# Transposing attention probabilities in blocks of 128 flat columns, with V spread by DMA and expert chunks two slots earlier

## What is computed

```python
q, k = rms_norm(q, qn_w), rms_norm(k, kn_w)
attn = softmax(einsum('bqhd,bkhd->bhqk', q, k) / sqrt(64))      # 64 x 4 x 256 x 77
x = einsum('bhqk,bkhd->bqhd', attn, v).reshape(b, lq, 256) @ Wfc + fc_b
...
expert_out = einsum('becd,edf->becf', expert_in, We)            # 8 experts, 256 x 256 each
out = einsum('btk,btkd->btd', w, gathered)                      # w: softmax over the two best
x = x + tanh(g) * out
```

## Time and profile before

| | |
|---|---|
| median of 3 runs | 1439.17 us (1435.26 to 1442.53) |
| the profiled execution | 1435.99 us, span 1434.3 us |
| busy: PE, DVE, ACT, POOL | 98%, 77%, 65%, 53% of the span |
| granted TensorE clock, mean | 0.987 (1.00 in the steady pairs) |
| largest group | expert matmuls, 3072 of 512 columns, 788.0 us |
| probability transposes (L1276) | 512 matmuls |
| attention matmuls (`pT`, `vz`) | 768 of 256 columns |
| DMA, mean | 30 GB/s |

### The profile page before, as it was taken

The page is one execution under the profiler, slowest core; times in us unless marked ns, Lnnn a source line. Parts: engine busy times, 40 slices in busy tenths (PEclk is TensorE's granted clock), DMA queues, the critical chain, the costliest instruction groups (busy, mean ns, idle before and its releaser), DMA issues. The chain is left out here.

```text
span 1434.3 us, 27347 instructions
## 1 busy us (share of the span) xinstructions
PE 1398.4 (98%) x8448; PEld 1176.7 (82%) x8448; DVE 1110.1 (77%) x3146; ACT 931.2 (65%) x2600; POOL 765.4 (53%) x915
## 2 busy tenths in 40 slices
PE   5799999999999999999999999999999999999998
PEld 4688888888888888888888888888888888888876
DVE  6677877877878777878777878777878778878763
ACT  6666667666667666667666667666677666676652
POOL 3344565555565555565545565545565545565544
PEclk7799999999999999999999999999999999999999
DMA  4001110101110100100101100001101011101000
GB/s 150 19 2 35 35 35 9 35 27 35 35 35 8 35 28 35 35 24 20 35 27 35 35 17 26 31 32 35 35 9 35 28 35 35 35 9 35 8 23 23
DMA packets 29074, 43.65 MB, mean 30 GB/s; under 512 B 4672, under 2 KB 12288, under 8 KB 28928
## 3 DMA queue, kind: packets, MB, share of 16 engines
q1 hardware_dynamic: 28928, 41.90, 8.6%
HBM read 25.11 MB, written 16.78 MB: 29 GB/s over the span
## 5 line engine op out<-in xcount | busy, mean ns | idle before, releaser
L314 PE MATMUL bkM<-we,x2T 128*128 128x512 f32 x3072 | 788.0, 398 | 5.0 <-DVE acc_v L1020 0.6
L314 PEld LDWEIGHTS bkM<-we,x2T 128*128 128x128 f32 x3072 | 551.8, 188 | 132.7 <-ACT a_out L640 17.5
L640 ACT ACTIVATE a_out<-bkM,gate 128x256 f32<-128x256 f32 x512 | 215.5, 476 | 163.5 <-PE bkM L314 159.6
L455 POOL TENSOR_TENSOR a_sum<-a_sum,a_out 128x256 f32<-128x256 f32 x256 | 187.7, 733 | 94.5 <-ACT a_out L640 62.7
L1020 DVE SCALAR_TENSOR_TENSOR acc_v<-bkM,gate,acc_v 128x256 f32<-128x256 f32 x384 | 185.4, 483 | 56.9 <-PE bkM L314 47.8
L411 POOL TENSOR_TENSOR rstd<-ve,minus_half 128x4 f32<-128x4 f32 x64 | 64.8, 1012 | 208.0 <-DVE ve L814 208.0
L411 POOL TENSOR_TENSOR q_r<-q_ve,minus_half 128x16 f32<-128x16 f32 x32 | 93.1, 2910 | 113.0 <-DVE q_ve L899 113.0
L442 POOL TENSOR_TENSOR probs<-probs,p_inv 128x308 f32<-128x308 f32 x128 | 91.4, 715 | 82.0 <-DVE p_inv L914 82.0
L411 POOL TENSOR_TENSOR k_r<-k_ve,minus_half 77x8 f32<-77x8 f32 x32 | 52.3, 1634 | 145.8 <-DVE k_ve L863 145.8
L545 ACT ACTIVATE xn<-x_sb,shift,rstd 128x256 f32<-128x256 f32 x128 | 66.5, 590 | 76.9 <-DVE shift L823 76.9
L460 POOL TENSOR_TENSOR y<-a_sum,acc_v 128x256 f32<-128x256 f32 x128 | 94.5, 738 | 17.3 <-issue 0.4
(11 more groups left out here) (177 smaller groups left out, 2888.6 us busy)
## 6 DMA issues: line engine op xcount, KB each, us to landing
x_sb<-in_x SPq DMA_DIRECT2D x32, 512.0 KB, 3.9
out<-y SPq DMA_DIRECT2D x64, 256.0 KB, 2.0
ctx_sb<-in_ctx SPq DMA_DIRECT2D x32, 154.0 KB
stage<-in_L_ffn_We SPq DMA_DIRECT2D x2, 1024.0 KB, 6.1
stage<-in_L_xattn_Wkv SPq DMA_DIRECT2D x1, 512.0 KB, 5.4
stage<-in_L_xattn_Wq SPq DMA_DIRECT2D x1, 256.0 KB, 5.5
stage<-in_L_xattn_Wfc SPq DMA_DIRECT2D x1, 256.0 KB, 3.9
bias_bc<-in_L_xattn_fc_b SPq DMA_DIRECT2D x1, 128.0 KB, 4.9
```

Of the source, the lines that this page charges most:

```text
L314: mm = nc.tensor.matmul(out, l, r, start=(i == 0), stop=(i == len(terms) - 1))
L455: nc.gpsimd.tensor_tensor(a, o[:, 0] if i == 1 else a, o[:, i], ALU.add).then_inc(a_summed.sem, 1)
L640: ins = nc.scalar.activation(a_out[:, t % 2, (e // 4) * 2 + i], bkM[1][:, i * D:(i + 1) * D], ACT.Copy, scale=gate[:, m.parity, t, e:e + 1])
```

## The change

Four things.

1. **Transposes.** The four heads' probabilities stand side by side in `probs`, 4 x 77 = 308 flat columns. They are padded to 384 (the padding is zeroed once) and transposed as 3 blocks of 128, whatever head a column is of. Flat column 77 h + k becomes a row of block c = (77 h + k) // 128. 12 transposes per pair instead of 16, each 128 x 128. `pT` is 128 x 384 per tile instead of 77 x 512.
2. **V.** A row of a block must meet the V row of the same head and key. ACT and DVE now write V's parts plainly (`v_nat`, 77 rows), and SP moves them into `vf` by six DMAs (`put_v`): each head's 77 rows, cut where a block ends, to the partitions where the block has them, in the 64 columns of that head; the rest of `vf` is zero from the start. Half 0 needs blocks 0 and 1, half 1 blocks 1 and 2, so each output is still two products of three terms.
3. **Attention by batch.** An output bank holds one batch with both halves (before: one half with both batches). TensorE runs both halves of batch 0 in slot 14, of batch 1 in slot 15, and the projection of a batch waits for that batch alone.
4. **Chunks two slots earlier.** In slot k runs chunk k + 2 of pair m, in slots 14 and 15 chunks 0 and 1 of pair p. Chunks 0 and 1 of the first pair move into `second_round`; the last step has 14 chunks. POOL's `finish_tile` of tiles 0 and 1 moves ahead accordingly.

```diff
+V_BLOCKS = ((0, 0), (1, 0), (1, 1), (2, 1))
+def v_pieces():
+    for h in range(H):
+        row = h * LK
+        while row < (h + 1) * LK:
+            c = row // P
+            end = min((h + 1) * LK, (c + 1) * P)
+            yield V_BLOCKS.index((c, h // 2)), row - c * P, row - h * LK, end - row, h
+            row = end
+def block_rows(c):
+    return min(P, HK - c * P)
...
-        vz = sb("vz", [LK, 2, BP, KC, 2 * P], F32R)
+        v_nat = sb("v_nat", [LK, 2 * BP, D], F32R)
+        vf = sb("vf", [P, 2 * BP, len(V_BLOCKS), P], F32R)
...
+        LEAD = 2
+        def chunk_of(k, m, p):
+            c = k + LEAD
+            return (m, c) if c < SLOTS else (p, c - SLOTS)
...
+            def put_v(f):
+                sp.wait_ge(v_lo.sem, v_lo.at(f))
+                sp.sem_inc(waits_alone, 1)
+                sp.wait_ge(o_ps.sem, o_ps.before(f))
+                sp.sem_inc(waits_alone, 1)
+                for block, row, k, n, h in V_PIECES:
+                    sp.dma_start(vf[row:row + n, :, block, (h % 2) * DH:(h % 2 + 1) * DH].bitcast(F32),
+                                 v_nat[k:k + n, :, h * DH:(h + 1) * DH].bitcast(F32)).then_inc(v_put.sem, 16)
...
                 if ahead:
                     load(ahead)
+                if f:
+                    put_v(f)
                 store(m, 0)
...
             def slots(m, p, f):
                 if f:
                     ln1(f)
+                if m:
+                    finish_tile(m, 0)
                 if p:
                     ln2(p)
                 if f:
                     k_rsqrt(f)
                 if m:
-                    finish_tile(m, 0)
+                    finish_tile(m, 1)
                 if f:
                     make_xb(f, 0)
                     q_rsqrt(f)
                     make_xb(f, 1)
                     make_xb(f, 3)
-                if m:
-                    finish_tile(m, 1)
...
-                copy(pT[:, 0, t // SUB, :, t % SUB], s_bank[t][0:LK, :].rearrange("k (h q) -> k h q", h=H)
-                     ).then_inc(pT_hi.sem, 1)
+                copy(pT[:, 0, t // SUB, :, t % SUB], p_chunks(t)).then_inc(pT_hi.sem, 1)
...
-                for h in range(H):
-                    tr = pe.transpose(s_bank[t][0:LK, h * P:(h + 1) * P], probs[:, t, h * LK:(h + 1) * LK],
-                                      ident[:])
+                for c in range(PC):
+                    tr = pe.transpose(s_bank[t][:, c * P:(c + 1) * P], probs[:, t, c * P:(c + 1) * P], ident[:])
...
             def attend(f, m, b, p):
-                pe.wait_ge(v_lo.sem, v_lo.at(f))
                 if m == 0:
+                    pe.wait_ge(v_put.sem, v_put.at(f))
+                    pe.wait_ge(pT_lo.sem, pT_lo.at(f, SUB * (b + 1)))
                     if p and b == 0:
                         pe.wait_ge(x2T_lo.sem, x2T_lo.at(p))
-                    pe.wait_ge(pT_lo.sem, pT_lo.at(f, SUB * (b + 1)))
-                elif p and b == 0:
-                    pe.wait_ge(gate_chain.sem, gate_chain.at(p))
-                mm = product(o_bank[m][:, b * LQ:(b + 1) * LQ], [
-                    ([vz[:, a, b, m, j * P:(j + 1) * P] for a in range(2)],
-                     [pT[:, a, b, 2 * m + j].rearrange("k s q -> k (s q)") for a in range(2)])
-                    for j in range(2)])
+                    elif p:
+                        pe.wait_ge(gate_chain.sem, gate_chain.at(p))
+                mm = product(o_bank[b][:, m * LQ:(m + 1) * LQ], [
+                    ([vf[0:rows, a * BP + b, block] for a in range(2)],
+                     [pT[0:rows, a, b, c].rearrange("k s q -> k (s q)") for a in range(2)])
+                    for block, (c, heads) in enumerate(V_BLOCKS) if heads == m
+                    for rows in (block_rows(c),)])
...
                 if k == 14 and f:
                     attend(f, 0, 0, p)
+                    attend(f, 1, 0, p)
                 if k == 15 and f:
                     attend(f, 0, 1, p)
-                    attend(f, 1, 0, p)
                     attend(f, 1, 1, p)
```

More of the change, by code:

```diff
@@ L571, in kv @@
                                      ).then_inc(k_sq_done.sem, 1)
-                act.wait_ge(o_ps.sem, o_ps.before(f))
-                copy(vz_heads(0, b), v_heads(b)).then_inc(v_hi.sem, 1)
+                act.wait_ge(v_put.sem, v_put.before(f))
+                copy(v_nat[:, b], v_cols(b)).then_inc(v_hi.sem, 1)
             def q(f, i):
@@ L643, in experts, with chunk @@
                 ins.then_inc(a_ready.sem, 1)
+            def chunk(k, m, p):
+                pair, c = chunk_of(k, m, p)
+                if pair:
+                    experts(pair, c)
             def slot(k, m, p, f, xn_made=False):
@@ L651, in slot @@
                         ctx_hi(f)
-                    if m:
-                        experts(m, k)
+                    chunk(k, m, p)
                 if k == 3:
@@ L667, in slot @@
                         ln2(p)
-                if k == 5 and m:
-                    experts(m, k)
+                if k == 5:
+                    chunk(k, m, p)
                 if k == 6:
@@ L1420, in second_round @@
                 positions(p)
-                attend(f, 0, 0, p)
-                attend(f, 0, 1, p)
-                attend(f, 1, 0, p)
-                attend(f, 1, 1, p)
+                moe(p, 0)
+                for b in range(BP):
+                    attend(f, 0, b, p)
+                    attend(f, 1, b, p)
+                moe(p, 1)
             def fill():
```

67 lines of the change are left out of this document (40 added, 27 removed).

## The result

The changed kernel takes 1446.87 us, the median of 8 runs (1446.29 to 1451.17); the kernel before, run beside it, takes 1437.59 us (8 runs, 1435.26 to 1442.53). The ratio is 1.0072, 95% interval 1.0056 to 1.0087: slower by 0.7%, where 0.5% can be told from no change. The runs of the kernel before fall mostly into two groups, near 1436 and near 1442.4 us (in later series near 1436 and 1443), and a median depends on how many fall into each. The forecast of 1429 us has the wrong sign, and the result lies above its range. The profiled execution of the changed kernel took 1446.31 us, its span is 1444.6 us at a granted clock of 0.989.

The account below looks back on a forecast made before the run. TensorE, 98% busy, bounds the kernel, beside a DVE chain as long as its own work from slot 10 to attention. Steady pairs -9.0, shift +0.2, fill -1.3 sum to -10.1 us; 1439.17 becomes 1429 us, range 1417 to 1439.

Parts of the forecast that it names:

- The attention products: TensorE's 24 attention matmuls of 256 columns per pair: contracting 128 or 52 rows instead of 77 costed at nothing.
- rival D: Transposes: a group's cost follows the loaded columns, +0.44 us per pair, +13 us, 1452 us; chance 3%.
- Transposes, -0.45 us on TensorE: Probability transposes: 16 become 12 per pair, 4 x 0.1125 = 0.45 us off TensorE; the wider load costs nothing.
- the estimate that the prediction worked out from the Trainium skill: Transposes' weight loads: 1.0 us before, 1.3 after if loads set the pace, costing 0.3 us per pair.
- Kept 0.30 of it, DVE binds: At the first attention matmul: TensorE meets DVE's second low part, so 0.30 of 0.45 us per pair is kept, 9.0 us.
- POOL's limit: Fourth transpose group: POOL's last normalisation keeps it from starting before about 850.5, putting attention at about 852.3.
- Stall before chunk 13: Chunk 13's weights waiting for ACT's evacuation: the 0.3 us stall may go, but TensorE only arrives earlier at the same wait.
- rival A: TensorE's path alone decides: DVE's chain shrinks too, 0.45 us and the 0.3 us stall both go, 1415.6 us; chance 8%.
- The shift +0.2: Chunks two slots earlier: no work moved in steady state; drain -2.8, fill 1.4 and about 2.2, attention gain 0.6: +0.2 us.
- the fill -1.3: First two pairs: transposes cost 0.215 us each there, three groups save 0.65 us per pair, -1.3 us.
- V by DMA hidden: SP's queue: six pieces, 5 to 10 us plus issues of about 0.4 each, under 25.5 us of cover; costed at nothing.
- the dear end: V's DMA at the upper packet price of 68 ns: 1,232 packets take 5.3 us on sixteen engines, 84 on one.

Follow-up runs that it names:

- the kernel with 128 rows: The changed kernel with its last block of 52 rows contracted over all 128 rows (zero padding): 1420.96 us against 1437.16, ratio 0.9878.
- the split kernel: The changed kernel with all blocks at 128 rows, and DVE's two low parts moved ahead of the last three gate instructions: 1412.08 us, ratio 0.9813.

## Why the prediction was wrong

The step that failed is in "The attention products": "I cost that at nothing: the columns are the same, and none of the rows above goes by the contracted rows". Its cost is 0.71 us per pair by the starts in the timeline and 0.78 us by the kernel with 128 rows, some 23 us in all by the spans and 26 by the medians; the prediction's sum held it at nothing. The reasoning had a gap that can be named. All rows quoted for it contracted 77 or 128 rows; for 52 I had no row near, and took the column count for the whole price instead of bounding it. The kernel before did have a nearer row, the logits' transposes of 16 rows at 0.34 us for four, which costs more than its columns explain.

The sentence behind it failed too: "boundaries with expert chunks are as many as before". I counted boundaries between tiles and not between kinds of product, and those went from none in the attention to four per pair. None of the rivals held such a mechanism: D priced the loaded columns of the transposes, and the only slower cases had 8% between them.

The Trainium skill has a page that speaks to it, and I had not drawn on it: "TensorEngine Tiling (Array Packing)", Key Properties, says that changing the tiling mode drains TensorE, and under Performance Considerations it puts contraction sizes of 64 or less under row tiling. The step between 64 and 77 rows and the 0.195 to 0.21 us per switch would fit that; that a product of 52 rows changes the mode in this kernel is argued, and no run here shows it. The Trainium skill ("TensorE: Matmul & The Clock Gate", LDWEIGHTS) also says that a weight load's time goes by columns and not by rows. The trace agrees for the load by itself, 0.18 us with 52 rows and 0.19 with 128; at the edges of the short block the load is not hidden all the same.

The other steps, in order. One more row is needed for them, the start of DVE's chain behind chunk 10 in the changed kernel:

```profile
809.60 0.48 DVE L1068 SCALAR_TENSOR_TENSOR acc_v<-bkM,gate,x 128x256 f32<-128x256 f32 x1 [1.00 <-PE bkM L339]
```

- **Transposes, -0.45 us on TensorE: right.** The first two groups of three start 0.36 us apart, 0.12 each. The wider load costs nothing; rival D falls. So does the estimate that the prediction worked out from the Trainium skill ("TensorE: Matmul & The Clock Gate", LDWEIGHTS).
- **Kept 0.30 of it, DVE binds: right in mechanism.** Low parts of 384 columns take 0.55 us, as forecast, and the attention starts 0.10 us behind the second. Moving DVE's gates gave 0.33 us per pair, which shows that DVE held it. With 128 rows the period is 42.82, 0.42 below before: the term was 0.12 us per pair too small. POOL's limit was nearer than I made it: it costs 0.34 us ahead of the fourth group.
- **Stall before chunk 13: "may well go", it went.** 0.36 us per pair, and as I had said TensorE waits elsewhere instead: for POOL ahead of the fourth group, and longer for DVE at the attention. From the start of DVE's chain at 809.60 to the attention at 816.94 it is 7.34 us, and 7.70 before (844.99 to 852.69). Of the 0.36, the two low parts give 0.26, the lag behind them 0.04 and the routing ahead of them 0.06. That last is all that came of rival A's shorter chain.
- **The shift +0.2, the fill -1.3: right within 1 us at the ends, with 2.3 us missed in the steady pairs.** Drain -2.7 (said -2.8), first positions -1.7. The first interval is 3.0 longer by the shift, as its terms said (1.4 + 2.2 - 0.6). That the shift moves no time in the steady state was wrong by 0.08 us per pair. POOL's delay of the second root did no visible harm.
- **V by DMA hidden: right, with a price off.** Six issues take 5.24 us on SP, 0.87 each and not 0.4. Nothing waited for them. The trace's packets show the landing: the 1,232 packets of 256 B start between 837.4 and 842.1 us at 18 ns each, where the dear end had 68, and the last of the six pieces has landed at 842.5, 18 us ahead of the next pair's attention. The move of V apart from the transposes was not tried by itself.

The sum without the failed term, -10.1 us, compares with -16 us in the median and -12.5 in the spans of the kernel with 128 rows. With the term, -10.1 + 30 x 0.78 = +13.3 us, against +9.3 measured. The baseline was off as well: three runs gave 1439.17, eight give 1437.59.

## What to carry to other kernels

Look at the contracted rows of neighbouring products, not only at their columns: a product of 64 rows or fewer among ones of 77 or more costs this kernel about 0.2 us at each side in the attention, and the zeros that pad it (to 96 or 128 rows in the attention, to 80 in the transposes) cost less than they save. So pad, or put all short products side by side, which no run here tried from the start. A busy share near 100% doesn't say that the time is work: compare start-to-start times of equal runs of matmuls across the kernel, and hold suspect the shape for which there is no row. And what a saving is worth is decided at the waits behind it: the same padding lengthened one wait for ACT by as much in both kernels, and gave 4.1 us only in the one where a later wait, for POOL, shrank with it.

## What the runs showed that I had not expected

- A switch between attention products of at most 64 and of more contracted rows costs 0.195 to 0.21 us, the same whether 4 or 12 of them stand in a pair; 52 and 64 rows pay it, 77, 96 and 128 don't. The transposes of 16 rows pay too: two edges gave 0.21 us net of wider transposes. It shows as TensorE busy, with the weight load starting at its own matmul. What the engine does in that time the trace doesn't say.
- Transposes of fp32 that contract 77 rows or more go by their moving columns: 0.11 us for 128, with 77 or 128 loaded; 0.055 to 0.062 for 77 and 80, with 128 and 80 loaded.
- The same small DVE instruction on 32 columns can take 0.19 us or 0.74: the last of the gates in the changed and in the split kernel, in nearly all pairs of each. The slow one (798.26) starts 0.04 us behind the start of a POOL addition and ends with it, the fast one (815.71) starts 0.06 us ahead of one; that this is the cause was not tried.
- SP needs 0.87 us on average to issue one piece of V (six in 5.24 us), from 256-byte runs in SBUF to SBUF, against 0.39 for the store of an output tile in the row behind them. The queue's packets go from the earlier trace rows's 28,928 to 70,144, and its share of the DMA engines only from 8.6% to 11.6%.
